# Second attention of a two-layer block: transposes interleaved with other matmuls on TensorE, and queries and keys split on GpSimd

## What is computed

```python
x = x + _L0_attn_ref(_layernorm(x), wq, wk, wv, wo)           # 32 heads of 128, 8 key heads, rotary
x = x + _L0_ffn_ref(_layernorm(x), gate_t, up_t, down_t, ...) # width 1792
x = x + _L1_attn_ref(_layernorm(x), w_qkv, b_qkv, w_out, b_out)
x = x + _L1_ffn_ref(_layernorm(x), A, B, Wr)                  # 64 experts of rank 16, top 16
```

```python
q, k, v = split(einsum('bsd,od->bso', x, w_qkv) + b_qkv)      # (2, 512, 32, 16) each
scores = einsum('bqhd,bkhd->bhqk', q, k) / sqrt(16) + slopes[head] * positions[key]
attn = softmax(where(causal, scores, -1e9))
out = einsum('bhqk,bkhd->bqhd', attn, v)
x = x + out @ w_out.T + b_out
```

## Time and profile before

| | |
|---|---|
| median of three runs | 1504.5 us |
| the profiled execution | 1505.23 us, span 1503.2 us |
| busy: TensorE, its weight loads | 1433.1, 1195.1 us |
| busy: VectorE, ScalarE, GpSimd | 1009.5, 857.5, 555.7 us |
| mean granted TensorE clock | 0.991 |

### The profile page before, as it was taken

The page is one execution under the profiler, slowest core; times in us unless marked ns, Lnnn a source line. Parts: engine busy times, 40 slices in busy tenths (PEclk is TensorE's granted clock), DMA queues, the critical chain, the costliest instruction groups (busy, mean ns, idle before and its releaser), DMA issues.

```text
span 1503.2 us, 25443 instructions
## 1 busy us (share of the span) xinstructions
PE 1433.1 (95%) x7696; PEld 1195.1 (80%) x7696; DVE 1009.5 (67%) x2538; ACT 857.5 (57%) x2184; POOL 555.7 (37%) x484
## 2 busy tenths in 40 slices
PE   5899999999999999999988999999789999988999
PEld 4788888888888888888867888888567777776787
DVE  7776667766777667666656333344688889889742
ACT  2676566655566556665653332220589989988310
POOL 5474464644645456454240000023161314116500
PEclk9999999999999999999999999999899999999999
DMA  4010110100100001000021111114434435461000
GB/s 171 8 50 15 29 43 21 28 21 28 35 21 28 28 28 35 14 28 7 1 71 43 63 60 45 42 36 78 75 84 76 96 69 102 78 144 57 1 22 35
DMA packets 37517, 71.97 MB, mean 48 GB/s; under 512 B 4993, under 2 KB 5377, under 8 KB 36865
## 3 DMA queue, kind: packets, MB, share of 16 engines
q1 hardware_dynamic: 29664, 55.35, 11.8%
q0 software_dynamic: 7776, 15.73, 7.1%
HBM read 60.58 MB, written 10.49 MB: 47 GB/s over the span
## 4 chain that ended last, share of the span: by engine, by line
PE 80%; ACT 6%; DVE 6%; issue 4%; DMA 2%; POOL 1%; DVEq 0%; ACTq 0%; SPq 0%; POOLq 0%
PE ps_up L66 9%; PE ps_up L65 9%; PE ps_up L64 9%; PE ps_gate L64 8%; PE ps_gate L66 8%; PE ps_gate L65 8%; PE ps_out L64 5%; PE ps_out L66 5%; PE ps_out L65 5%; PE ps_out L556 4%; PE ps_up L1853 2%; ACT a_probs L2123 2%; PE ps_out L1841 2%; PE ps_gate L1828 2%; ACT a_probsT_hi L2132 2%
## 5 line engine op out<-in xcount | busy, mean ns | idle before, releaser
L822 ACT ACTIVATE a_probs<-a_probs,a_least 128x512 f32<-128x512 f32 (+3 forms) x256 | 143.0, 560 | 162.2 <-DVE a_least L683 157.2
L405 POOL TENSOR_TENSOR a_rotated<-a_by_cos,a_by_sin 128x512 f32<-128x512 f32 x80 | 103.7, 1296 | 224.9 <-DVE a_by_sin L706 222.7
L691 DVE TENSOR_TENSOR a_probsT_lo<-ps_out,a_probsT_hi 128x512 fp32r<-128x512 f32 (+3 forms) x256 | 118.5, 484 | 67.9 <-ACT a_probsT_hi L830 66.7
L830 ACT CAST a_probsT_hi<-ps_out 128x512 fp32r<-128x512 f32 (+3 forms) x256 | 101.5, 427 | 92.4 <-PE ps_out L556 91.6
L2123 ACT ACTIVATE a_probs<-a_probs,a_least 128x128 f32<-128x128 f32 (+3 forms) x256 | 142.2, 560 | 3.4 <-issue 1.6
L1992 DVE CUSTOM_DVE_ANT_0 a_probs<-ps_gate,a_causal 128x128 f32<-128x128 f32 (+3 forms) x256 | 117.1, 486 | 33.6 <-PE ps_gate L1828 20.7
L882 ACT ACTIVATE a_probs<-a_probs,a_inverse 128x128 f32<-128x128 f32 (+3 forms) x256 | 123.1, 553 | 9.6 <-DVE a_inverse L724 8.6
L415 POOL TENSOR_TENSOR a_query_lo<-a_rotated,a_query_hi 128x512 fp32r<-128x512 f32 x64 | 82.7, 1292 | 107.8 <-ACT a_query_hi L842 107.8
L683 DVE CUSTOM_DVE_ANT_0 a_probs<-ps_out,a_causal 128x512 f32<-128x512 f32 (+2 forms) x192 | 101.2, 551 | 29.6 <-PE ps_out L66 29.6
L64 PE MATMUL ps_up<-a_wo_hi,a_attended_hi 128*128 128x512 f32 x278 | 113.4, 408 | 2.3 <-issue 1.4
L64 PE MATMUL ps_gate<-xT_hi,a_wq_hi 128*128 128x512 f32 x256 | 108.9, 425 | 1.6 <-DVE a_values_lo L719 1.6
(11 more groups left out here) (279 smaller groups left out, 4082.5 us busy)
## 6 DMA issues: line engine op xcount, KB each, us to landing
a_raw<-in_wq SPq DMA_DIRECT2D x36, 256.0 KB, 2.7
a_raw<-in_wo SPq DMA_DIRECT2D x36, 256.0 KB, 2.6
a_stacked_q<-a_spill_q POOLq DMA_DIRECT2D x48, 128.0 KB, 4.5
a_stacked_k<-a_spill_k POOLq DMA_DIRECT2D x24, 256.0 KB, 4.6
f_raw<-in_gate SPq DMA_DIRECT2D x14, 256.0 KB, 2.7
f_raw<-in_up SPq DMA_DIRECT2D x14, 256.0 KB, 2.9
f_raw<-in_down SPq DMA_DIRECT2D x14, 256.0 KB, 3.5
a_raw<-in_wk SPq DMA_DIRECT2D x12, 256.0 KB, 2.8
```

The costliest lines, as they stand in the source:

```text
L691: nc.vector.tensor_tensor(probsT[1][:, t % 2, 0:w], ps_turn[:, t % 2, 0:w], probsT[0][:, t % 2, 0:w].bitcast(F32), ALU.subtract).then_inc( ...
L822: nc.scalar.activation(tile, tile, ACT.Exp, bias=least[:, slot, i:i + 1], scale=-1.0, accum_out=total[:, slot, i:i + 1]).then_inc(exp_done, 1)
```

## The change

- TensorE's step is written in another order. Transposes of the turning unit stand between the value matmuls of the attended unit and the scores, nearly one by one. Part 0 of the attention is the third instruction of the step, waits for the high halves alone (`turned_hi`), and part 1 waits for the low halves.
- From chunk 0 on, both halves of a query or key block are made by GpSimd (`split_operand`), ahead of its read-back. ScalarE rounds such blocks only for those ahead of chunk 0, and VectorE makes only their low halves. The low half of the query block of step (-1, 14) is made by VectorE a step later, in (0, 0).
- Before SyncE fetches the weights of the last part, it also waits until the last keys have been read back.

```diff
@@ -1689,6 +1689,7 @@
         sp.wait_ge(query_out, 2 * 16 * 2 * CHUNKS1)
         sp.wait_ge(keys_out, 2 * 16 * 2 * CHUNKS1)
+        sp.wait_ge(stacked_k_in, 16 * DMAS_K * 2 * CHUNKS1)
         moe.fetch_down(sp, (0, 1))
@@ -1719,11 +1720,23 @@
+        def split_operand(c, s):
+
+            what, count = SIDE1[s % 8], operand_count(c, s)
+            src, (hi, lo), done = (biased_q, query, query_out) if what == "query" else (biased_k, keys, keys_out)
+            wait(pool, operand_split, count - 1)
+            wait(pool, done, 2 * 16 * period(c, s))
+            pool.wait_ge(side_read, side_count(c, s))
+            nc.gpsimd.tensor_tensor(hi[:], src[:], zeros[:], ALU.add).then_inc(operand_hi, 1)
+            pool.wait_ge(operand_hi, count)
+            nc.gpsimd.tensor_tensor(lo[:], src[:], hi[:].bitcast(F32), ALU.subtract).then_inc(operand_split, 1)
+
         def chunk(c):
             more = not isinstance(c, int) or c < CHUNKS1 - 1
             first = isinstance(c, int) and c == 0
+            split_operand(c, 0)
             if first:
                 read_back(pool, c, 0)
@@ -1740,6 +1753,7 @@
             if more:
                 for s in (6, 8, 14):
+                    split_operand(c, s)
                     read_back(pool, c, s)
@@ -1828,34 +1845,45 @@
+        def attend(attending, part, k):
...
+            if k == 0:
+                if part == 0:
+                    if j == 0:
+                        wait(pe, side_read, side_count(cu, 3) if b else side_count(cu - 1, 11))
+                    wait(pe, attend_read, n)
+                    wait(pe, turned_hi, 3 * n + 3)
+                else:
+                    wait(pe, turned_split, 3 * n + 3)
@@ -1895,21 +1923,25 @@
+            turn(turning, 0, [0, 1])
+            attend(attending, 0, 0)
+            score(scoring, 0)
+            attend(attending, 0, 1)
+            score(scoring, 1)
+            turn(turning, 0, [2])
+            attend(attending, 0, 2)
+            turn(turning, 0, [3])
+            attend(attending, 0, 3)
+            attend(attending, 1, 0)
+            turn(turning, 1, [0])
+            attend(attending, 1, 1)
+            turn(turning, 1, [1])
+            attend(attending, 1, 2)
+            turn(turning, 1, [2])
+            attend(attending, 1, 3)
+            turn(turning, 2, [0, 1, 2])
+            score(scoring, 2)
+            score(scoring, 3)
@@ -2048,9 +2080,9 @@
-            if side1 in ("query", "keys") and isinstance(c1, int) and c1 < 0:
+            if side1 in ("query", "keys") and isinstance(c1, int) and c1 < 0 and s1 < STEPS1 - 2:
                 split_operand(c1, s1)
-            if side2 in ("query", "keys") and not (isinstance(c2, int) and c2 < 0):
+            if side2 == "query" and isinstance(c2, int) and (c2, s2) == (-1, STEPS1 - 2):
                 split_operand(c2, s2)
@@ -2178,7 +2210,7 @@
-            if side1 in ("query", "keys"):
+            if side1 in ("query", "keys") and isinstance(c1, int) and c1 < 0:
                 round_operand(c1, s1)
```

More of the change, by code:

```diff
@@ L1819, in make_last_out, with score @@
             product(nc, last_banks[t], [x[:, t * P:(t + 1) * P] for x in attended], [x[:] for x in wo], True, True).then_inc(last_made, 1)
-        def score(cu, u, i):
+        def score(scoring, i):
+            if not scoring:
+                return
+            cu, u = scoring
             n, b, j = STEPS1 * cu + u, u // HPC, u % HPC
@@ L1829, in score, with turn @@
                              stacked_k[:, b, j // 2, 0:P * (i + 1)], start=True, stop=True).then_inc(score_made, 1)
-        def turn(cu, u, t):
+        def turn(turning, t, blocks):
+            if not turning:
+                return
+            cu, u = turning
             n = STEPS1 * cu + u
[L1834 to L1842, removed]
@@ L1844, in attend @@
-        def attend(cu, u, part):
-            n, b, j = STEPS1 * cu + u, u // HPC, u % HPC
[L1847 to L1858, removed]
+            if 0 in blocks:
+                if t == 0:
+                    wait(pe, exp_done, 4 * n + 4)
+                wait(pe, turned_split, 3 * n - 2 + t)
@@ new lines, in turn @@
+            of_tile = [(k, i) for k in ((t,) if t < 2 else (2, 3)) for i in range(k, QT)]
+            for block in blocks:
+                k, i = of_tile[block]
+                at = SCORE_AT[i] + k * P
+                to = KEY_AT[k] - TURNED_AT[t] + (i - k) * P
+                mm = nc.tensor.transpose(ps_turn[:, t, to:to + P], probs[:, u % 4, at:at + P], m.ident[:])
+                if block == len(of_tile) - 1:
+                    mm.then_inc(turned, 1)
+        def attend(attending, part, k):
+            if not attending:
+                return
+            cu, u = attending
+            n, b, j = STEPS1 * cu + u, u // HPC, u % HPC
+            if k == 0:
[6 more added lines that the diff above has]
+                    wait(pe, turned_split, 3 * n + 3)
+            mm = nc.tensor.matmul(
+                ps_attend[0:2 * HD1, k * P:SEQ], values[:, b, k, j].rearrange("p h d -> p (h d)"),
+                probsT[part][:, u % 2, KEY_AT[k]:KEY_AT[k] + SEQ - k * P],
+                start=part == 0 and k == 0, stop=part == 1 and k == QT - 1)
+            if part == 1 and k == QT - 1:
+                mm.then_inc(attend_made, 1)
```

## The result

The changed kernel takes 1514.45 us, median of three runs (1514.12 to 1516.77), against 1504.5 before: a ratio of 1.0068 with a 95% interval of 1.0045 to 1.009. Forecast were 1513 us and a range of 1496 to 1522. The profiled execution took 1514.45 us, with a span of 1512.8.

What follows compares the result with a forecast made beforehand. TensorE bounds most steps before; afterwards a loop through TensorE and ScalarE: 61 steps at 4.75 us plus smaller terms, 320.3, plus 1 is 321.3 against 313.3; 1505.2 + 8.0 - 0.7 gives 1512.5, say 1513 us, range 1496 to 1522.

Steps and rivals of the forecast that it cites:

- the loop: Second attention: value matmul, last transpose, rounding, exponentials, gather, next value matmul; sets a step's least time, 4.75 us (4.66 to 4.86).
- The first rival: Second attention: ScalarE keeps ahead, TensorE's work bounds, minus 9 us, three long steps shrink: 1482 us; chance 0.10.
- The one with hidden transposes: TensorE in the second attention: five transposes ahead of another matmul cost 0.06 us each, 16 us less, near 1497; chance 0.06.
- the loop's first term: TensorE, first value matmul to start of last transpose: matmuls 1.34 us plus seven transposes 0.76, sum 2.10 us.
- Exponential 2 to the start of the gather: 1259.18 to 1260.50, 1.32: ScalarE's stretch of the loop from exponential 2 to the gather's start, taken as 1.32 us a step.
- TensorE-bound steps: Steps 5, 6, 13 and 14, where TensorE's own work is above the loop: 12 x 0.17 = 2 us.
- mask waits: Scores 2 and 3 wait for VectorE's masks behind divisions in steps 1, 5, 9, 13: 2 us a chunk kept, 8.
- loop turn: Turn of the program loop over chunks in the second attention: costs 1.6 us.
- hold: Step (0, 5): VectorE's division meets the end of GpSimd's eight additions; 1 us added, not the 4.4 it costs now.
- The signs: Profile signs expected afterwards: chunk times, TensorE busy time, waits, short (-1, 15), no long chunk 3 step, clock near 1.0.
- The low half at (-1, 15): VectorE's query low half moves behind that step's masks; the step falls from 8.3 to 3.6 us.
- The lock in chunk 0: Step (0, 5): VectorE's division and GpSimd's additions exclude each other; the division, later now, meets their end: 1 us.

Runs made afterwards that it cites:

- the faster order with gaps: Changed kernel with TensorE's order of before, plus GpSimd waiting for each of its eight bias additions before issuing the next: 1501.02 us, ratio 0.9963.
- the first experiment: Changed kernel with TensorE's order of before, its other parts kept: 1499.13 us, ratio 0.9965 to the kernel before.

## Why the prediction was right

**The interleaving is worth nothing on TensorE and costs the loop: right.** The part alone costs 21 us, the figure that the prediction gave the loop, and cutting the loop in two ways brought plain steps to 4.58 and 4.30 us. The first rival ("ScalarE keeps its lead") falls with the rows of step (3, 6), where TensorE waits twice. The one with hidden transposes falls with the loop's first term, 2.13 us, where it would have made some 1.84. That the part alone costs just those 21 us is partly chance, since the stalls changed under it; chunks 1 and 2, without stalls, grew by 4.8 and 4.1 us, against 4.6 and 3.8 in the changed kernel. The small saving on TensorE was as counted: step (1, 6), without a wait, goes from its first transpose to its side work in 2.84 us (1187.12 to 1189.96), for 2.98 less 0.15.

**The loop's length: right in kind, short by 0.14 us.** The failed term is "Exponential 2 to the start of the gather: 1259.18 to 1260.50, 1.32". I read it from step (2, 4). In the kernel before, step (1, 7) shows the usual case, timeline of ScalarE:

```profile
1194.49 0.62 ACT L2123 ACTIVATE a_probs<-a_probs,a_least 128x384 f32<-128x384 f32 x1
...
1195.93 0.57 ACT L2140 COPY a_gathered<-ps_up 32x512 f32<-32x512 f32 x1
```

That is 1.44 us. In the changed kernel only the gathers of steps 0, 4, 8 and 12, which carry one wait more in the program, start 0.12 us sooner. In chunk 1 of the changed kernel a loop with such a gather takes 4.82 us and the next one 4.95, by the first value matmuls of steps (1, 8) to (1, 10):

```profile
1197.34 0.41 PE L1881 MATMUL ps_up<-a_probsT_hi,a_values 128*32 128x512 f32 x1 [0.27 <-ACT a_gathered L2172]
...
1202.16 0.41 PE L1881 MATMUL ps_up<-a_probsT_hi,a_values 128*32 128x512 f32 x1
...
1207.11 0.41 PE L1881 MATMUL ps_up<-a_probsT_hi,a_values 128*32 128x512 f32 x1
```

In chunks 0 and 3, which are not in the loop of the program, they take 4.73 and 4.90. The mean over all is 4.89, and 61 x 0.14 makes 8.5 us that the sum lacked.

**TensorE-bound steps, mask waits, loop turn and hold: too much.** These were 2 + 8 + 1.6 + 1 = 12.6 us. What is left of 321.9 after 61 x 4.89, the two first steps (3.58 and 4.54, forecast 3.6 and 4.5) and the 10.8 of the extra copies is 4.7. Masks held the scores' weight loads for 1.4 us over chunks 1 and 2 in place of 6.6:

```profile
PEld ps_out L1863 <- DVE a_probsT_lo L2032: 3.8, 4, 1.0
...
PEld ps_gate L1845 <- DVE a_least L2024: 1.4, 8, 0.2
```

With the longer step VectorE had mostly caught up. The four waits for a low half stand ahead of T0 in steps 4 and 12, and cost nothing by themselves: the transpose there waited 0.73 us for the exponentials, which ended some hundredths later.

```profile
1175.88 0.43 PE L1863 MATMUL ps_out<-ident,a_probs 128*128 128x128 f32 x2 [0.73 <-ACT a_probs L2155]
```

What is above the loop lies mostly in steps 5 and 13, with the divisions, which take 5.36 to 5.46 us from value matmul to value matmul in chunks 0 to 2. An error of +8 and one of -8 cancel. The total is that near only by this, which is luck; the mechanism and the stalls at (-1, 15) and (3, 5) are what was right.

**The signs: mixed.** Chunks 1 and 2 took 83.1 and 83.4 us where "80 to 82" was written, with TensorE busy 76.6 and 77.0 and not "well under 76". The waits were named for "most steps", but over those 32 steps the profile lists them 12 times each:

```profile
PE ps_out L1863 <- ACT a_probs L2155: 6.7, 12, 0.8
...
PE ps_up L1881 <- ACT a_gathered L2172: 2.4, 12, 0.3
```

The rest came: no `a_result` above 1.24 us, no long step in chunk 3, a granted clock of 1.00. The limit of 4.6 us for a step holds only from value matmul to value matmul, where the shortest is 4.72; from T0 to T0 some are 4.5, as T0 is not in this loop.

**The low half at (-1, 15) and SyncE's wait: right in their steps.** The first step takes 3.6 us as forecast, the stall of 3.9 us is gone, and step (3, 5) takes 4.5 us, for the 4.75 I counted. Alone each gave the whole kernel only about 2 us; by the traces step (0, 5) and later steps took a part back.

**Operands on GpSimd at nothing: wrong when alone**, by 4 us, for a reason the prediction had looked away from: an earlier block starts GpSimd's additions earlier. It had "The block is then in place no later than before", and a block that comes sooner was not followed on. The trace shows that it did this in step (0, 5); the 1.3 us at (3, 5) have no shown cause.

**The lock in chunk 0: half of the cause.** The prediction costed it at 1 us, and the division took 0.8 us longer than its usual 0.43, because the loop made the steps slow enough. That the query weights' split waits behind the same additions stood in the program and was missed. In the changed kernel it held a weight load of step (0, 5) for 0.4 us, by the waits in 1098.8 to 1104.5 us; in the faster order with gaps it was 4.9.

```profile
PEld ps_out L64 <- POOL a_wq_lo L1714: 0.4, 1, 0.4
```

## What to carry to other kernels

Before interleaving two jobs on the busiest engine, follow each buffer once around all engines in their list order: the first consumer moved earlier and the last producer moved later both lengthen the same loop, and a loop 0.5 us above the engine's own work costs that in every step. To shorten it, move an instruction ahead of the point where the other engine's list waits, not behind it, and look for the second loop just below. When a stall is taken away and the time stays, look at what else waits on the same engine: here the division and a weight split stood behind the same eight additions.

## What the runs showed that I had not expected

- The granted clock was below 1.00 in steps with a long stall of TensorE. It was 0.70 in the 11.5 us step (0, 5) of the first experiment, 1.00 in the same step once it took 5.3 us, and 1.00 in all four chunks of the changed kernel. A stall of 4.9 us was followed by matmuls 0.43 us apart at a granted clock of 0.50, which is 1.2 GHz, against 0.23; the six of that step cost 1.2 us more.
- A division on VectorE lasted 0.43 to 5.36 us by its distance to the next gap on GpSimd, and gaps of some 0.1 us between the additions cut it from 5.21 to 1.08.
- A gather with one more semaphore wait in the program started 0.12 us sooner behind the exponential than one without. No run here tells why.
